# Flip and rotation of the Q and K projection issued one item later, with two qb slots

## The chip, the cores and the metric

The kernel runs on the 8 cores of one Trainium2 chip. Each core computes one batch element; the cores exchange nothing. The metric is the device time of the slowest core in microseconds.

## The reference

Two transformer layers over x of shape (8, 2048, 1024). Cut to what matters here, layer 1's attention:

```python
xn = _layernorm(x, axis=-1)
q = jnp.einsum('bsm,hmd->bshd', xn, W_Q) + b_Q      # 32 heads of 32
k = jnp.einsum('bsm,hmd->bshd', xn, W_K) + b_K
v = jnp.einsum('bsm,hmd->bshd', xn, W_V) + b_V
q = _apply_rotary(q, sin, cos, 32)   # x*cos + flip(x)*sin
k = _apply_rotary(k, sin, cos, 32)
# 16 virtual keys and values, masked softmax, out-projection
```

`flip` swaps the two halves of each head's 32 features, with a minus sign on one. Ahead of this lie layer 0 (a Taylor-feature attention and a mixture of 8 experts of width 4096, every expert computed for every token); behind it layer 1's feed-forward with ternary weights.

## The kernel before

All stages are written out in order by one Python program; each of the engines (TE is TensorE, VE VectorE, SE ScalarE, GE GpSimd's queue, SY SyncE's queue) runs its own instructions strictly in the order written. `barrier()` makes all five wait for everything issued so far. `use_bank` makes TensorE wait until the last reader of that PSUM bank is done. `mm.mark` and `vv.mark` raise a semaphore at the end of a TensorE or VectorE instruction, and `wait` on the returned token waits for that count.

`l1_attn` begins, after a barrier, with the Q and K projection, L908 to L971. xnT, the normalised input, lies in SBUF as 8 tiles of 128 features by 2048 tokens. `which` is 0 for Q and 1 for K. For each, a 4 MB weight matrix is loaded in one DMA from the POOL queue into Wb, converted to bf16 (L920; the helper's line is L224). The second load waits until all matmuls on the first are done (t_Wuse, L966). Then 32 items follow: 8 blocks a2 of 128 output features by 4 chunks cch of 512 tokens. One item is:

- L929: eight matmuls 128x128 by 128x512 that add up in PSUM bank 0 or 1 (tile pA), in turn
- L936 (Q) or L941 (K), VectorE: the eviction, adding the bias (and scaling Q) into the bf16 buffer qb, of which there is one. It waits for the matmuls and for the rotation of the item before, the last reader of qb
- L949: one matmul of qb with the constant pflip, into bank 2 or 3 (tile pB)
- L954: rt1 = qb * cos; L957: rt2 = flipped (in PSUM) * sin; L961: rt1 + rt2 into qrotT or krotT. They wait for L949

A VectorE drain stands ahead of L936/L941, L954 and L961. Each item's instructions are issued completely before those of the next. After the 64 items a small DMA loads the virtual keys (no wait of its own), a barrier follows, and then the V projection (L996, L1000, L1005), the attention proper (L1068 to L1114) and the feed-forward (L1196, L1210) run.

Of the kernel before, what the change touches and what calls it, by code (L numbers as in the profile page):

```python
# [9 lines left out]
BF16 = mybir.dt.bfloat16  # L10
AX = mybir.AxisListType.X
OP = mybir.AluOpType
# [3 lines left out]
DT = 8  # L16
# [5 lines left out]
L1QSC = 32.0 ** -0.5  # L22
# [84 lines left out]
def build(T=2048, upto=99, debug=(), l0sub=9):  # L107
    NT = T // 128
    NCH = T // 512
# [14 lines left out]
    wqf1 = dt("L1_WQ", [D, D], F32, kind="ExternalInput").ap()  # L124
    wkf1 = dt("L1_WK", [D, D], F32, kind="ExternalInput").ap()
# [37 lines left out]
    def sbl(st, name, shape, ty):  # L163
        _uniq[0] += 1
        return st.enter_context(nc.sbuf_tensor(f"{name}_{_uniq[0]}", list(shape), ty))

    xnT = st_xn.enter_context(nc.sbuf_tensor("xnT", [128, DT, T], BF16, side="right"))
    acc = st_acc.enter_context(nc.sbuf_tensor("acc", [128, NT, D], F32, side="right"))

    consts = {nm: es.enter_context(nc.sbuf_tensor("s_" + nm, [p_, f_], ty))  # L170
              for nm, (p_, f_, ty) in CSHAPES.items()}
# [6 lines left out]
    bq_c = es.enter_context(nc.sbuf_tensor("bq_c", [128, 8], F32))  # L178
    bk_c = es.enter_context(nc.sbuf_tensor("bk_c", [128, 8], F32))
# [6 lines left out]
    PS = [pA[:, 0:512], pA[:, 512:1024], pB[:, 0:512], pB[:, 512:1024],  # L186
          pC[:, 0:512], pC[:, 512:1024], pD[:, 0:512], pD[:, 512:1024]]
    bank_free = [None] * 8
# [3 lines left out]
    gw = Sem(es, nc, "gw", dma=True)  # L192
# [7 lines left out]
    mm = Sem(es, nc, "mm")  # L200
    vv = Sem(es, nc, "vv")
    sc = Sem(es, nc, "sc")
# [7 lines left out]
    tk = {}  # L210
    final_outs = []

    with es, nc.Block() as block:
        @block.sync
        def _(sync_unused):
            TE = Eng(nc.tensor)
            VE = Eng(nc.vector)
            SE = Eng(nc.scalar)
            GE = Eng(nc.gpsimd)
            SY = Eng(nc.sync)  # L220

            def dma(q, sem, out, in_, deps=(), **kw):
                q.wait(*deps)
                return sem.mark(q.raw.dma_start(out=out, in_=in_, **kw), 16)  # L224

            def use_bank(bk):
                TE.wait(bank_free[bk])
# [21 lines left out]
            with ExitStack() as st0:  # L249
# [22 lines left out]
                for a in range(DT):  # L272
                    VE.raw.tensor_scalar(out=wq_b[:, a, :], in0=wqf[:, a, 0:128],
                                         scalar1=gamma_c[:, a:a + 1], scalar2=QSC,
                                         op0=OP.mult, op1=OP.mult)
                    tk["wfold"] = vv.mark(VE.raw.tensor_scalar(
                        out=wkv_b[:, a, :], in0=wqf[:, a, 128:384],
                        scalar1=gamma_c[:, a:a + 1], scalar2=None, op0=OP.mult))
                with ExitStack() as st00:
                    wrtmp = sbl(st00, "wrtmp", (128, DT, 8), F32)  # L280
                    for a in range(DT):
                        small_transpose(wrT[:, a, :], wrtmp[:, a, :], a % 2, 8, 128,
                                        deps=(t_wr,))
                    VE.raw.drain()
                    tk["wr"] = vv.mark(VE.raw.tensor_copy(wr_b[:], wrtmp[:]))
                for e in range(8):
                    small_transpose(b1row[:, e, :], b1c0[:, e, :], 2 + e % 2, 32, 128,
                                    deps=(t_b1r,))
# [613 lines left out]
            def l1_attn():  # L902
                st_l1 = ExitStack()
                qrotT = sbl(st_l1, "qrotT", (128, 8, T), BF16)
                krotT = sbl(st_l1, "krotT", (128, 8, T + VKV), BF16)
                v_ext = sbl(st_l1, "v_ext", (128, NT + 1, 32, 65), BF16)
                with st_l1:
                    with ExitStack() as st:  # L908
                        sincos = sbl(st, "sincos", (128, 2, T), BF16)
                        Wb = sbl(st, "Wqk", (128, DT, D), BF16)  # L910
                        qb = sbl(st, "qb", (128, 512), BF16)
                        rt1 = sbl(st, "rt1", (128, 512), BF16)
                        rt2 = sbl(st, "rt2", (128, 512), BF16)
                        tk["sc"] = dma(GE, gd, sincos[:, 0, :], sin_in)
                        tk["sc"] = dma(GE, gd, sincos[:, 1, :], cos_in)
                        t_W = None
                        t_Wuse = None
                        t_qb_used = None
                        for which in range(2):
                            t_W = dma(GE, gw, Wb[:], (wqf1 if which == 0 else wkf1)  # L920
                                      .rearrange("(a p) m -> p a m", p=128), deps=(t_Wuse,))
                            dstT = qrotT if which == 0 else krotT
                            for a2 in range(8):
                                for cch in range(NCH):
                                    bk = (a2 * NCH + cch) % 2
                                    use_bank(bk)
                                    TE.wait(t_W)
                                    for a in range(DT):
                                        t_pq = mm.mark(TE.raw.matmul(  # L929
                                            PS[bk], lhsT=Wb[:, a, a2 * 128:(a2 + 1) * 128],  # L930
                                            rhs=xnT[:, a, cch * 512:(cch + 1) * 512],
                                            start=(a == 0), stop=(a == DT - 1)))
                                    VE.wait(t_pq, t_qb_used)
                                    VE.raw.drain()
                                    if which == 0:
                                        t_evq = vv.mark(VE.raw.tensor_scalar(  # L936
                                            out=qb[:], in0=PS[bk],
                                            scalar1=bq_c[:, a2:a2 + 1], scalar2=L1QSC,
                                            op0=OP.add, op1=OP.mult))
                                    else:  # L940
                                        t_evq = vv.mark(VE.raw.tensor_scalar(  # L941
                                            out=qb[:], in0=PS[bk],
                                            scalar1=bk_c[:, a2:a2 + 1], scalar2=None,
                                            op0=OP.add))
                                    bank_free[bk] = t_evq
                                    bk2 = 2 + (a2 * NCH + cch) % 2
                                    use_bank(bk2)
                                    TE.wait(t_evq, tk["consts"])
                                    t_fl = mm.mark(TE.raw.matmul(  # L949
                                        PS[bk2], lhsT=consts["pflip"][:], rhs=qb[:],  # L950
                                        start=True, stop=True))
                                    VE.wait(t_fl, tk["sc"])
                                    VE.raw.drain()
                                    VE.raw.tensor_tensor(  # L954
                                        out=rt1[:], in0=qb[:],
                                        in1=sincos[:, 1, cch * 512:(cch + 1) * 512], op=OP.mult)
                                    VE.raw.tensor_tensor(  # L957
                                        out=rt2[:], in0=PS[bk2],
                                        in1=sincos[:, 0, cch * 512:(cch + 1) * 512], op=OP.mult)
                                    VE.raw.drain()  # L960
                                    t_rot = vv.mark(VE.raw.tensor_tensor(  # L961
                                        out=dstT[:, a2, cch * 512:(cch + 1) * 512],
                                        in0=rt1[:], in1=rt2[:], op=OP.add))
                                    bank_free[bk2] = t_rot
                                    t_qb_used = t_rot
                            t_Wuse = mm.tok()  # L966
                        tk["rotdone"] = vv.tok()
                        tk["vk"] = dma(GE, gd, krotT[:, :, T:T + VKV],
                                       vk1.rearrange("(a p) m -> p a m", p=128),
                                       allow_slow_non_contiguous=True)  # L970
                        barrier()  # L971

                    with ExitStack() as st:
# [8 lines left out]
                                       deps=(t_vz, t_vo))  # L982
                        t_WVuse = None
                        for half in range(2):
# [3 lines left out]
                                       deps=(t_WVuse,))  # L988
                            for kvt in range(NT):
                                for hc2 in range(2):  # L990
                                    hc = half * 2 + hc2
                                    bk = 4 + (kvt * 2 + hc2) % 4
                                    use_bank(bk)
                                    TE.wait(t_WV, t_bv)
                                    for a in range(DT):
                                        TE.raw.matmul(  # L996
                                            PS[bk], lhsT=xnT[:, a, kvt * 128:(kvt + 1) * 128],
                                            rhs=WVb[:, a, hc2 * 512:(hc2 + 1) * 512],
                                            start=(a == 0), stop=False)
                                    t_pv = mm.mark(TE.raw.matmul(  # L1000
                                        PS[bk], lhsT=ones_row_bf[:],
                                        rhs=bv_r[0:1, hc * 512:(hc + 1) * 512],
                                        start=False, stop=True))
# [19 lines left out]
                    with ExitStack() as st:  # L1023
# [20 lines left out]
                        for cch in range(NCH):  # L1044
# [6 lines left out]
                                        deps=(t_wob_used,))  # L1051
                            for a2 in range(8):
# [4 lines left out]
                                for p in range(nsteps + 1):  # L1057
                                    if p < nsteps:
# [4 lines left out]
                                        sl = p % 2  # L1063
                                        for hh in range(4):
# [5 lines left out]
                                                lhsT=krotT[hb:hb + 32, a2,  # L1070
                                                           kvt * 128:kvt * 128 + rows],
                                                rhs=qrotT[hb:hb + 32, a2,
                                                          cch * 512:(cch + 1) * 512],
                                                start=True, stop=True,
# [255 lines left out]
```

How the kernel before makes its waits and increments, by code:

```python
    def mark(self, instr, n=1):  # L77
        instr.then_inc(self.h, n)
        self.v += n
        return (self, self.v)
# [10 lines left out]
    def wait(self, *deps):  # L91
        for d in deps:
            if d is None:
                continue
            if isinstance(d, (list, tuple)) and d and isinstance(d[0], (list, tuple, type(None), Sem)) \
                    and not (len(d) == 2 and isinstance(d[0], Sem)):
                self.wait(*d)
                continue
            sem, val = d
            if sem.dma:
                val = sem.v
            if val > self.seen.get(sem, 0):
                self.raw.wait_ge(sem.h, val)
                self.seen[sem] = val
```

## Time and profile before

| | us |
|---|---|
| median of 3 runs | 8478.11 |
| the three runs | 8478.11, 8134.01, 8685.17 |
| the profiled execution | 8134.01 |
| its span on the slowest core (core 7) | 8132.4 |
| spans of the eight cores | 8082.8 to 8132.4 |

The profile is of the execution that took 8134.01 us, on its slowest core. PE is TensorE's matmuls, PEld its weight loads, DVE VectorE, ACT ScalarE, POOL GpSimd. A matmul's end is modelled; successive matmuls overlap, so the distance from start to start tells their rate. Idle time of an engine matters only where the chain of waits runs through it.

### The profile page before, as it was taken

The page shows a single profiled execution, that of the slowest core. Times are in us where ns is not written, and L with a number is a line of the kernel's source. Part 1 is how long each engine was busy: PE and PEld are TensorE (multiplying, and loading weights), DVE is VectorE, ACT ScalarE, POOL GpSimd, SP SyncE. Part 2 cuts the span into 40 slices and gives each one's busy share as a digit, 9 for nine tenths or more (in the row PEclk, how much of TensorE's full clock was granted, in tenths as well). Part 3 has the DMA queues.
Part 4 walks back from the last instruction along what each step waited for, and adds up shares of the span by engine and source line. Part 5 has one row for each costly group of instructions (what it writes and reads, how often), then busy time and mean ns, then how long its engine had stood idle before and what let it go on. Part 6 is the DMA issues. An engine that isn't in the chain of part 4 may idle for free.

```text
span 8132.4 us, 72354 instructions; the slowest of 8 cores (8082.8 to 8132.4 us)
## 1 busy us (share of the span) xinstructions
PE 6021.8 (74%) x25392; PEld 2488.6 (31%) x25392; DVE 2372.5 (29%) x4977; ACT 1739.0 (21%) x2768; POOL 152.4 (2%) x177
## 2 busy tenths in 40 slices
PE   3354899999998877887877777936656567676687
PEld 1111344444433333333333333412211122221233
DVE  4633222222222222222222222246343422323000
ACT  1000111111111111111111111100043546474121
POOL 0000000000000000000000000000000000000000
PEclk9555899999999988998988888959866777777898
DMA  1000323323322122112132112020112020201423
GB/s 51 4 0 1 64 45 63 63 45 65 83 55 52 37 52 57 37 34 55 29 62 47 42 39 51 10 57 11 21 36 32 1 32 1 32 1 16 128 66 81
DMA packets 165181, 336.80 MB, mean 41 GB/s; under 512 B 13171, under 2 KB 54940, under 8 KB 162404
## 3 DMA queue, kind: packets, MB, share of 16 engines
q0 software_dynamic: 107888, 221.31, 15.6%
q1 hardware_dynamic: 56948, 110.85, 4.3%
q8 instruction: 220, 3.60, 0.2%
q14 instruction: 125, 1.02, 0.0%
HBM read 445.96 MB, written 46.14 MB: 61 GB/s over the span
## 4 chain that ended last, share of the span: by engine, by line
PE 66%; DMA 11%; DVE 9%; ACT 6%; issue 6%; DVEq 2%; SPq 0%; POOL 0%; ACTq 0%; POOLq 0%
PE pA L706 22%; PE pB L722 11%; PE pC L722 11%; ACT expT L1077 4%; PE pA L1196 3%; DMA denM<-den_stg 2%; DMA wbuf<-L_W 2%; DMA w1t_sc<-buf 2%; PE pB L1210 1%; PE pA L929 1%; PE pC L1210 1%; PE pD L620 1%; PE pC L1099 1%; PE pA L1068 1%; DVE zT L1114 1%
## 5 line engine op out<-in xcount | busy, mean ns | idle before, releaser
L706 PE MATMUL pA<-xnT,W1q 128*128 128x512 bf16 x8192 | 1820.2, 384 | 0.0
L711 ACT ACTIVATE h<-pA,b1c 128x512 bf16<-128x512 f32 x1024 | 703.8, 687 | 3713.7 <-PE pA L706 3713.7
L706 PEld LDWEIGHTS pA<-xnT,W1q 128*128 128x128 bf16 x8192 | 808.1, 99 | 986.2 <-issue 46.3
L736 DVE SCALAR_TENSOR_TENSOR acc<-pB,G,acc 128x512 f32<-128x512 f32 x512 | 383.5, 751 | 2240.7 <-PE pB L722 1640.5
L722 PE MATMUL pB<-W2q,h 128*128 128x512 bf16 x4096 | 936.8, 379 | 124.9 <-ACT h L711 120.0
L722 PE MATMUL pC<-W2q,h 128*128 128x512 bf16 x4096 | 937.6, 379 | 0.0
L722 PEld LDWEIGHTS pB<-W2q,h 128*128 128x128 bf16 x4096 | 383.5, 98 | 637.7 <-issue 207.5
L1077 ACT ACTIVATE expT<-pA,shcol 128x512 bf16<-128x512 f32 (+1 forms) x704 | 462.3, 736 | 414.9 <-PE pA L1068 358.5
L736 DVE SCALAR_TENSOR_TENSOR acc<-pC,G,acc 128x512 f32<-128x512 f32 x512 | 384.0, 751 | 537.9 <-PE pC L722 349.9
L722 PEld LDWEIGHTS pC<-W2q,h 128*128 128x128 bf16 x4096 | 390.3, 98 | 482.1 <-issue 29.0
L1084 DVE TENSOR_TENSOR expT<-expT,s_masks 128x512 bf16<-128x512 bf16 (+1 forms) x640 | 270.4, 425 | 809.6 <-ACT expT L1077 791.9
L771 PE MATMUL pD<-s_ident,wbuf 128*128 128x128 f32 x512 | 116.3, 383 | 495.7 <-DMA w2t_sc<-buf 168.8
L1077 ACT ACTIVATE expT<-pB,shcol 128x512 bf16<-128x512 f32 (+1 forms) x704 | 465.7, 749 | 0.0
L1068 PE MATMUL pA<-qrotT,krotT 32*128 32x512 bf16 (+1 forms) x704 | 191.9, 469 | 343.8 <-DVE zT L1114 309.5
L1068 PE MATMUL pB<-qrotT,krotT 32*128 32x512 bf16 (+1 forms) x704 | 272.1, 460 | 59.7 <-ACT expT L1077 49.2
L1099 PE MATMUL pC<-expT,v_ext 128*65 128x512 bf16 (+1 forms) x704 | 282.9, 487 | 3.8 <-DVE expT L1084 1.5
L1099 PE MATMUL pD<-expT,v_ext 128*65 128x512 bf16 (+1 forms) x704 | 262.7, 454 | 11.8 <-DVE expT L1084 11.6
L1196 PE MATMUL pA<-xnb,w1tb 128*128 128x512 bf16 x1024 | 223.2, 381 | 43.9 <-DMA w1tb<-w1t_sc 43.5
L776 DVE TENSOR_SCALAR ttmp<-pD,thrc 128x128 bf16<-128x128 f32 x512 | 144.3, 344 | 354.3 <-PE pD L771 345.2
L771 PEld LDWEIGHTS pD<-s_ident,wbuf 128*128 128x128 f32 x512 | 83.1, 196 | 527.1 <-issue 524.5
L1068 PEld LDWEIGHTS pA<-qrotT,krotT 32*128 32x128 bf16 (+1 forms) x704 | 41.7, 94 | 542.8 <-issue 541.2
L355 PE MATMUL pA<-s_ident,ln_xtmp 128*128 128x128 f32 x256 | 84.9, 435 | 159.9 <-DVE ln_xtmp L347 128.3
(253 smaller groups left out, 3621.9 us busy)
## 6 DMA issues: line engine op xcount, KB each, us to landing
W1q<-L_W POOLq DMA_DIRECT2D x32, 2048.0 KB, 18.7
W2q<-L_W POOLq DMA_DIRECT2D x32, 2048.0 KB, 32.4
wbuf<-L_W SPq DMA_DIRECT2D x32, 1024.0 KB, 12.0
w2tb<-w2t_sc POOLq DMA_DIRECT2D x8, 4096.0 KB, 17.5
wbuf<-L_W SPq DMA_DIRECT2D x32, 512.0 KB, 10.5
wbuf<-L_W SPq DMA_DIRECT2D x64, 256.0 KB, 4.9
WOb<-L_WO POOLq DMA_DIRECT2D x8, 2048.0 KB, 15.4
o<-stg POOLq DMA_DIRECT2D x64, 256.0 KB, 4.1
```

The source lines that it names most:

```text
L706: t_p1 = mm.mark(TE.raw.matmul(PS[bk], lhsT=W1q[:, s, a, ft * 128:(ft + 1) * 128], rhs=xnT[:, a, tq * 512:(tq + 1) * 512], start=(a == 0), ...
L711: bank_free[bk] = sc.mark(SE.raw.activation(h1[:, ft, :], PS[bk], ACT.Relu, bias=b1c0[:, e, qq * 8 + ft:qq * 8 + ft + 1]))
L722: ins = TE.raw.matmul(PS[bk], lhsT=h1[:, ft, ts_ * 128:(ts_ + 1) * 128], rhs=W2q[:, s, ft, dch * 512:(dch + 1) * 512], start=(ft == 0), st ...
L736: bank_free[bk] = vv.mark(VE.raw.scalar_tensor_tensor(out=aslc, in0=PS[bk], scalar=G[:, tq * 4 + ts_, e:e + 1], in1=aslc, op0=OP.mult, op1 ...
L771: tr = mm.mark(TE.raw.transpose(PS[bk][:, i4 * 128:(i4 + 1) * 128], s_ap, ident32[:]))
L776: VE.raw.tensor_scalar(out=ttmp[:, i4, :], in0=PS[bk][:, i4 * 128:(i4 + 1) * 128], scalar1=thrc[:, thc + 1:thc + 2], scalar2=None, op0=OP. ...
L1068: t_s = mm.mark(TE.raw.matmul(PS[hh][0:rows, :], lhsT=krotT[hb:hb + 32, a2, kvt * 128:kvt * 128 + rows], rhs=qrotT[hb:hb + 32, a2, cch * 5 ...
L1077: t_ex = sc.mark(SE.raw.activation(expT[0:rows, 2 * hh + sl, :], PS[hh][0:rows, :], ACT.Exp, bias=shcol[0:rows, :]))
L1084: t_ex = vv.mark(VE.raw.tensor_tensor(out=expT[0:rows, 2 * hh + sl, :], in0=expT[0:rows, 2 * hh + sl, :], in1=s_masks[0:rows, delta // 128 ...
L1099: t_z[hh] = mm.mark(TE.raw.matmul(PS[4 + hh][0:65, :], lhsT=v_ext[0:rows, kvt, h, :], rhs=expT[0:rows, 2 * hh + sl, :], start=(pz == 0), s ...
L1196: t_p1 = mm.mark(TE.raw.matmul(PS[bk], lhsT=w1tb[:, a, fc * 128:(fc + 1) * 128], rhs=xnb[:, a, tq * 512:(tq + 1) * 512], start=(a == 0), s ...
L1210: TE.raw.matmul(PS[bk], lhsT=hbuf[:, fc, qt * 128:(qt + 1) * 128], rhs=w2tb[:, ws, fc, :], start=(fc == 0), stop=False)
```

## The change

The 64 items are put in one list, and the loop runs over p from 0 to 64. At p it issues the eight matmuls and the eviction of item p, and then the flip matmul and the rotation of item p-1. qb gets two slots, p%2; t_pq, t_evq and t_qb_used are kept per slot. The second weight load is issued at p = 32 and waits for the last matmul of L929 on the first weights, not for all of TensorE's work. rt1 and rt2 stay single. The operations, their shapes and their number are the same.

```diff
-                        qb = sbl(st, "qb", (128, 512), BF16)
+                        qb = sbl(st, "qb", (128, 2, 512), BF16)
...
-                        for which in range(2):
-                            t_W = dma(GE, gw, Wb[:], (wqf1 if which == 0 else wkf1)
-                                      .rearrange("(a p) m -> p a m", p=128), deps=(t_Wuse,))
-                            dstT = qrotT if which == 0 else krotT
-                            for a2 in range(8):
-                                for cch in range(NCH):
-                                    bk = (a2 * NCH + cch) % 2
...
+                        items = [(w_, a2_, c_) for w_ in range(2)
+                                 for a2_ in range(8) for c_ in range(NCH)]
+                        nit = len(items)
+                        half = nit // 2
+                        for p in range(nit + 1):
+                            if p < nit:
+                                which, a2, cch = items[p]
+                                if p % half == 0:
+                                    t_W = dma(GE, gw, Wb[:],
+                                              (wqf1 if which == 0 else wkf1)
+                                              .rearrange("(a p) m -> p a m", p=128),
+                                              deps=(t_Wuse,))
+                                sl = p % 2
+                                bk = p % 2
+                                use_bank(bk)
+                                TE.wait(t_W)
+                                for a in range(DT):
+                                    t_pq[sl] = mm.mark(TE.raw.matmul(
+                                        PS[bk], lhsT=Wb[:, a, a2 * 128:(a2 + 1) * 128],
+                                        rhs=xnT[:, a, cch * 512:(cch + 1) * 512],
+                                        start=(a == 0), stop=(a == DT - 1)))
+                                if p == half - 1:
+                                    t_Wuse = t_pq[sl]
+                                VE.wait(t_pq[sl], t_qb_used[sl])
+                                VE.raw.drain()
+                                if which == 0:
+                                    t_evq[sl] = vv.mark(VE.raw.tensor_scalar(
+                                        out=qb[:, sl, :], in0=PS[bk],
+                                        scalar1=bq_c[:, a2:a2 + 1], scalar2=L1QSC,
+                                        op0=OP.add, op1=OP.mult))
...
+                                bank_free[bk] = t_evq[sl]
+                            if p >= 1:
+                                which, a2, cch = items[p - 1]
+                                sl1 = (p - 1) % 2
+                                dstT = qrotT if which == 0 else krotT
+                                bk2 = 2 + (p - 1) % 2
+                                use_bank(bk2)
+                                TE.wait(t_evq[sl1], tk["consts"])
+                                t_fl = mm.mark(TE.raw.matmul(
+                                    PS[bk2], lhsT=consts["pflip"][:], rhs=qb[:, sl1, :],
+                                    start=True, stop=True))
+                                VE.wait(t_fl, tk["sc"])
+                                VE.raw.drain()
+                                VE.raw.tensor_tensor(
+                                    out=rt1[:], in0=qb[:, sl1, :],
+                                    in1=sincos[:, 1, cch * 512:(cch + 1) * 512], op=OP.mult)
+                                VE.raw.tensor_tensor(
+                                    out=rt2[:], in0=PS[bk2],
+                                    in1=sincos[:, 0, cch * 512:(cch + 1) * 512], op=OP.mult)
+                                VE.raw.drain()
+                                t_rot = vv.mark(VE.raw.tensor_tensor(
+                                    out=dstT[:, a2, cch * 512:(cch + 1) * 512],
+                                    in0=rt1[:], in1=rt2[:], op=OP.add))
+                                bank_free[bk2] = t_rot
+                                t_qb_used[sl1] = t_rot
```

## Rows read from the trace of the kernel before

**Rows 1.** The page: busy times, chain by line, a group (us busy, mean ns | idle before).
```profile
PE 6021.8 (74%) x25392; PEld 2488.6 (31%) x25392; DVE 2372.5 (29%) x4977; ACT 1739.0 (21%) x2768; POOL 152.4 (2%) x177
...
PE pA L706 22%; PE pB L722 11%; PE pC L722 11%; ACT expT L1077 4%; PE pA L1196 3%; DMA denM<-den_stg 2%; DMA wbuf<-L_W 2%; DMA w1t_sc<-buf 2%; PE pB L1210 1%; PE pA L929 1%; PE pC L1210 1%; PE pD L620 1%; PE pC L1099 1%; PE pA L1068 1%; DVE zT L1114 1%
...
L736 DVE SCALAR_TENSOR_TENSOR acc<-pB,G,acc 128x512 f32<-128x512 f32 x512 | 383.5, 751 | 2240.7 <-PE pB L722 1640.5
```

**Rows 2.** Timeline, items 0, 2, 34, 63: start, length, engine, operation, count [idle before <-releaser].
```profile
5464.99 3.57 PE L929 MATMUL pA<-xnT,Wqk 128*128 128x512 bf16 x8 [44.77 <-DMA Wqk<-L_WQ]
...
5476.85 0.75 DVE L936 TENSOR_SCALAR qb<-pA,bq_c 128x512 bf16<-128x512 f32 x1 [0.28 <-PE pA L929]
...
5599.42 0.75 DVE L941 TENSOR_SCALAR qb<-pA,bk_c 128x512 bf16<-128x512 f32 x1 [0.28 <-PE pA L929]
...
5693.41 0.75 DVE L941 TENSOR_SCALAR qb<-pA,bk_c 128x512 bf16<-128x512 f32 x1 [0.28 <-PE pA L929]
...
5695.94 0.43 DVE L961 TENSOR_TENSOR krotT<-rt,rt 128x512 bf16<-128x512 bf16 x1
```

**Rows 3.** Waits, 5400 to 5700 us: who <- for whom, us in total, times, longest.
```profile
POOL Wqk L224 <- PE pB L949: 124.3, 1, 124.3
...
DVE rt L954 <- PE pB L949: 42.8, 63, 0.9
PE pB L949 <- DVE qb L936: 37.0, 32, 1.5
```

**Rows 4.** Timeline of one steady item of Q and the next eviction.
```profile
5499.80 0.75 DVE L936 TENSOR_SCALAR qb<-pA,bq_c 128x512 bf16<-128x512 f32 x1 [0.28 <-PE pA L929]
...
5500.70 0.38 PE L949 MATMUL pB<-qb,s_pflip 128*128 128x512 bf16 x1 [1.13 <-DVE qb L936]
...
5500.91 1.89 PE L929 MATMUL pA<-xnT,Wqk 128*128 128x512 bf16 x8
5501.23 0.42 DVE L954 TENSOR_TENSOR rt<-qb,sincos 128x512 bf16<-128x512 bf16 x1 [0.67 <-PE pB L949]
5501.57 0.68 DVE L957 TENSOR_TENSOR rt<-pB,sincos 128x512 bf16<-128x512 f32 x1
5502.33 0.42 DVE L961 TENSOR_TENSOR qrotT<-rt,rt 128x512 bf16<-128x512 bf16 x1
5503.03 0.75 DVE L936 TENSOR_SCALAR qb<-pA,bq_c 128x512 bf16<-128x512 f32 x1 [0.28 <-PE pA L929]
```

**Rows 5.** Timeline of the last items of Q and the load of K's weights.
```profile
5564.78 0.75 DVE L936 TENSOR_SCALAR qb<-pA,bq_c 128x512 bf16<-128x512 f32 x1 [0.28 <-PE pA L929]
...
5570.89 0.43 DVE L961 TENSOR_TENSOR qrotT<-rt,rt 128x512 bf16<-128x512 bf16 x1 [0.43 <-issue]
5571.47 0.75 DVE L936 TENSOR_SCALAR qb<-pA,bq_c 128x512 bf16<-128x512 f32 x1 [0.16 <-DVE qrotT L961]
...
5572.37 0.38 PE L949 MATMUL pB<-qb,s_pflip 128*128 128x512 bf16 x1 [1.36 <-DVE qb L936]
...
5573.30 0.89 POOL L224 DMA_DIRECT2D Wqk<-L_WK  x1 [124.29 <-PE pB L949]
...
5587.26 3.57 PE L929 MATMUL pA<-xnT,Wqk 128*128 128x512 bf16 x8 [14.52 <-DMA Wqk<-L_WK]
```

**Rows 6.** Groups by line and form, 5400 to 5700 us: rotation and eviction (us busy, mean ns).
```profile
L957 DVE TENSOR_TENSOR rt<-pB,sincos 128x512 bf16<-128x512 f32 x64 | 43.8, 684 | 0.0
...
L936 DVE TENSOR_SCALAR qb<-pA,bq_c 128x512 bf16<-128x512 f32 x32 | 24.0, 751 | 58.8 <-PE pA L929 58.7 <-DVE qrotT L961 0.2
```

**Rows 7.** Windows: us, busy (and count) by engine, granted clock (PEclk), DMA share, GB/s.
```profile
5475.00:5568.00 93.00, 60.48 (x260) 23.17 (x258) 63.10 (x115) 0.00 (x0) 0.00 (x0) 1.00 0.00 1
...
5764.00:5820.00 56.00, 56.00 (x235) 20.57 (x235) 18.05 (x26) 0.00 (x0) 0.00 (x0) 1.00 0.00 1
```

More of the change, by code:

```diff
@@ L917, in l1_attn @@
                         t_Wuse = None
-                        t_qb_used = None
-                        for which in range(2):
-                            t_W = dma(GE, gw, Wb[:], (wqf1 if which == 0 else wkf1)
-                                      .rearrange("(a p) m -> p a m", p=128), deps=(t_Wuse,))
-                            dstT = qrotT if which == 0 else krotT
-                            for a2 in range(8):
-                                for cch in range(NCH):
-                                    bk = (a2 * NCH + cch) % 2
[L926 to L966, printed above, removed]
@@ new lines, in l1_attn @@
+                        t_pq = [None, None]
+                        t_evq = [None, None]
+                        t_qb_used = [None, None]
+                        items = [(w_, a2_, c_) for w_ in range(2)
[28 more added lines that the diff above has]
+                                        op0=OP.add, op1=OP.mult))
+                                else:
+                                    t_evq[sl] = vv.mark(VE.raw.tensor_scalar(
+                                        out=qb[:, sl, :], in0=PS[bk],
+                                        scalar1=bk_c[:, a2:a2 + 1], scalar2=None,
+                                        op0=OP.add))
+                                bank_free[bk] = t_evq[sl]
[23 more added lines that the diff above has]
+                                t_qb_used[sl1] = t_rot
```

## The prediction

> **What bounds the kernel now.** I read the page first. TensorE is busy 6021.8 of 8132.4 us, and the chain that ended last runs mainly through the expert matmuls L706 and L722, with L929, a line of the changed loop, at 1% [rows 1]. So the changed stage is a small part, and the first question is how long it is. The timeline answers: its first matmul starts at 5464.99 us and its last rotation ends at 5695.94 + 0.43 = 5696.37 us [rows 2], a stage of 231.4 us, 2.8% of the span. Barriers stand on both sides of it, so nothing else of the kernel overlaps it, and what it loses or gains moves the end one for one.
>
> Next the stage's waits: TensorE waits 37.0 us for the 32 evictions of Q before their flips (as long again for K), and VectorE waits 42.8 us for the flips [rows 3]. That is a ring. One steady item shows it [rows 4]. Call the eviction E, the flip F, the rotation's three operations R1, R2, R3, the eight matmuls mm. E starts at 5499.80, F at 5500.70, mm of the next item at 5500.91 for 1.89 us, and the next E at 5503.03. The period is 3.23 us = 0.90 (E and hand-off) + 0.21 (F until mm can start) + 1.89 (mm) + 0.23 (hand-off). The rotation, 5501.23 to 5502.75, lies beside mm and ends 0.28 us before E. TensorE idles 1.13 us in each item because F sits at once behind its own E.
>
> **The change part by part.** (a) *F and R go one item later.* TensorE's order becomes mm(p), F(p-1), mm(p+1), F(p); VectorE's E(p), R(p-1), E(p+1), R(p). The ring is opened: mm(p+1) needs E(p-1) (its bank, and F(p-1) ahead of it in the queue), not E(p). Two engine sums then compete.
>
> TensorE: the eight matmuls take 1.89 us including the end of the last, 0.379 long, so they start (1.89 - 0.38)/7 = 0.216 us apart; nine of them are 1.94 us per item.
>
> VectorE, from start to start: E to R1 0.75 + 0.08 = 0.83 (the 0.08 is the gap a drain leaves between R2, 0.68 long, and R3, which starts 0.76 after it); R1 to R2 0.34; R2 to R3 0.76 [rows 4]; R3 to the next E 0.58, from the one place where E waited for the rotation in front of it, 5570.89 to 5571.47 [rows 5]. That wait stays: slot p%2 was last read by R(p-2), which is the operation directly ahead of E(p). Sum 2.51 us. VectorE is the bound, and the period falls from 3.23 to 2.51.
>
> Is the loop free of other rings at 2.51? Put E(p-1) at 0. It is seen at 0.90; F(p-1) starts, mm(p+1) starts at 1.11 and ends at 3.00; E(p+1) is due at 5.02. R1(p-1) is due behind E(p), at 2.51 + 0.83 = 3.34, and F needs 0.53 us until R1 can start (5500.70 to 5501.23), so it is ready at 1.43. Slack is 1.8 us or more on both sides: that is the cover of F and mm. Without it, each would again cost its 1.1 us per item.
>
> Do VectorE's operations keep their durations when matmuls write other banks beside them? R2 reads PSUM beside mm in all but the last item of each half and has 684 ns throughout [rows 4, 6]; E reads PSUM with TensorE idle now, 751 ns. The expert stage has 512 accumulations from PSUM at the same 751 ns while TensorE works nearly without a gap [rows 1]. I take no stretch.
>
> Sum over periods. Items 2 to 29 of Q: 5564.78 - 5476.85 = 87.9 us, becoming 27 x 2.51 = 67.8, gain 20.2. Items 2 to 31 of K: 5693.41 - 5599.42 = 94.0, becoming 29 x 2.51 = 72.8, gain 21.2 [rows 2, 5].
>
> (b) *Starts at the low clock.* The first matmuls of each half run at the lower of TensorE's two levels, 1.2 GHz: eight take 3.57 us, starts (3.57 - 0.58)/7 = 0.427 apart [rows 2]. TensorE then no longer waits for E between the first groups. Q: mm(0), mm(1), F(0), about three low and five fast matmuls of mm(2), hand-offs: 3.42 + 3.42 + 0.43 + 1.28 + 1.08 + 0.39 = 10.0 us until E(2) against 5476.85 - 5464.99 = 11.9; gain 1.9. K likewise with F(31) in front: 10.4 against 5599.42 - 5587.26 = 12.2; gain 1.8 [rows 2, 5]. The moment of the rise is taken as in the profile, some 8 to 9 us in.
>
> (c) *The load of WK.* It now waits for the last matmul of Q, not for the last flip. Before: E(29) at 5564.78, load issued at 5573.30, 8.52 us. After: mm(31) follows F(29), so it ends 0.90 + 0.21 + 1.89 = 3.00 us after E(29); the queue needs 5573.30 - (5572.37 + 0.38) = 0.55. Gain 8.52 - 3.55 = 5.0 us [rows 5]. The load itself takes 5587.26 - 5573.30 = 13.96 us as before, with nothing else moving. F(31) now stands behind mm(32) and so behind this load; R(31) is late by 14 us, but only E(33) needs its slot, and it is done by then. The virtual-key load behind WK on the POOL queue moves with it and has no reader before the barrier.
>
> (d) *The end.* One more rotation trails the last E: 0.83 + 0.34 + 0.76 + 0.50 + 0.34 + 0.76 + 0.43 = 3.96 us, against 5696.37 - 5693.41 = 2.96 now. Loss 1.0. The wider qb costs nothing but memory.
>
> Sum: 20.2 + 21.2 + 1.9 + 1.8 + 5.0 - 1.0 = 49.1 us. The profiled execution took 8134.0 us, 1.6 beyond its span; 8134.0 - 49.1 = **8085 us**. The median of the three runs shown, 8478.1, is 344 us higher than the one profiled; the sum is for an execution like the profiled one, and the ratio, 0.994, carries over.
>
> *Bounds of the period.* Unseen so far are E followed by a drain and a wait already met, and 60 back-to-back items. Lower end: durations alone, less the 0.08 by which R2 starts before R1 ends, 0.75 + 0.42 + 0.68 + 0.42 - 0.08 = 2.20 us, gain 49.1 + 56 x 0.31 = 66.5. Upper end: a hand-off as if from another engine, 0.28 us, on both sides of E: 0.75 + 0.28 + 0.34 + 0.76 + 0.42 + 0.28 = 2.83, gain 49.1 - 56 x 0.32 = 31.2. I take 2.51 since its two gaps come from this loop's own instructions.
>
> **The rivals.** *A. VectorE has no gaps beyond its durations.* The period is 0.75 + 0.42 + 0.68 + 0.42 = 2.28 us, the gain 49.1 + 56 x 0.23 = 62 us, the time 8072. For it: these four durations are fixed within 2 ns. Against: R3 to E took 0.58, not 0.42 [rows 5]. The Trainium skill, VectorE: DVE Perf Modes, "The DRAIN you can't avoid", states this rule: a next operation starts when the pipe is empty, and a semaphore costs nothing extra; by it the time would be 8072. The trace agrees only in part: R2 starts 0.08 us before R1 ends, and a semaphore of the operation in front did cost 0.16.
>
> *B. Dear waits on VectorE*, the upper end above: 8103. For it: each item has three waits and three drains in a strict queue. Against: a drain shows 0.08.
>
> *C. The change doesn't overlap.* If something keeps mm(p+1) from starting until E(p) is seen, F and R moved but the ring stays at about 3.2 us; 8134. For it: nothing I find; bank p%2 is freed by E(p-2), and both flip banks by R(p-3). Against: the same matmuls run without pause in the V projection, TensorE busy 56.00 of 56.00 us [rows 7].
>
> *D. TensorE falls to 1.2 GHz: slower.* Nine matmuls at 0.427 make 3.84 us per item, above today's 3.23. All 64 items: 32 x 3.42 + 30 x 0.43 + 0.7 + 14.0 + 32 x 3.84 + 3.3 = 263 us against 231.4, so 8134 + 32 = 8166. It decides from the point where the mean item passes 3.23: (3.23 - 2.51)/(3.84 - 2.51) = 54% of the items at the low level. Against: the stage's granted clock is 1.00 (2.4 GHz) with TensorE paused 1.13 us in every item, and 1.00 again where it is packed [rows 7]; the change lies between the two. The Trainium skill, TensorE: Matmul & The Clock Gate, "A second HAM failure mode: psum-queue depth-cycling", warns that short idle moments between 512-column groups cycling through banks can make the clock swing. If it held here the time would go toward 8166; the 1.00 of the present loop, which has longer pauses, speaks against it.
>
> **How the numbers follow.** Main case 0.60 (8085), A 0.12 (8072), B 0.17 (8103), C 0.07 (8134), D 0.04 (8166). Main, A and B hold 0.89, between 8068 and 8103. An execution's other 7900 us also vary; the two longest cores lie at 8131.9 and 8132.4, the others down to 8082.8. I widen to **8055 to 8128**. About 2%, 163 us, is what a measurement of this kernel can tell from no change. Even a TensorE-bound loop (1.94 us) would gain 7.7 + 87.9 + 94.0 - 56 x 1.94 = 81 us, and D loses 32, so all cases are within 2%: faster 0.02, same 0.96, slower 0.02 for what I have not seen.
>
> **What would show it.** Period of E to E 2.51 us (A: 2.28, B: 2.83, C: 3.2, D: 3.8); VectorE idle below 0.3 us per item, no longer waiting for flips; TensorE's wait for E of item p-1 about 0.6 us per item; WK issued some 81 us after the first matmul, not 108; stage 182 us instead of 231; granted clock 1.00. The prediction is wrong if E stretches beyond 0.75 us beside matmuls, if R1 still waits for F, or if a later stage is longer by tens of us.

## The result and the profile after

| us | before | after |
|---|---|---|
| profiled execution | 8134.0 | 8081.9 |
| its span, slowest core (7) | 8132.4 | 8080.1 |
| median of 13 runs | 8469.9 | 8131.8 |
| ratio after / before | | 0.9935, 95% interval 0.9911 to 0.9958 |
| the changed stage, core 7 | 231.4 | 181.4 |
| the changed stage, mean of 8 cores | 229.7 | 180.9 |

The change is faster by 0.65%, clear of the noise but well inside 2%. In some executions of either kernel the cores of one die, or of both, ran at a lower granted clock for part of the time and took up to 10% longer; the ratio leaves those out, the two medians do not.

In the changed kernel the matmuls are L938, the eviction L947 (Q) and L952 (K), the flip L964, the rotation L969, L972 and L976. First its chain by line, from the page: the expert matmuls still lead, and the line of the changed loop, L929 with 1% before, is no longer in the list.

```profile
PE pA L706 22%; PE pB L722 11%; PE pC L722 11%; ACT expT L1091 4%; PE pA L1210 3%; DMA denM<-den_stg 2%; DMA wbuf<-L_W 2%; DMA w1t_sc<-buf 2%; PE pB L1224 2%; PE pC L1224 1%; PE pD L620 1%; PE pC L1113 1%; PE pA L1082 1%; DVE zT L1128 1%; DVE den_stg L1125 1%
```

The timeline of one steady item and the next eviction, core 7, answers [rows 4]:

```profile
5489.25 0.75 DVE L947 TENSOR_SCALAR qb<-pA,bq_c 128x512 bf16<-128x512 f32 x1 [0.16 <-DVE qrotT L976]
5490.09 0.42 DVE L969 TENSOR_TENSOR rt<-qb,sincos 128x512 bf16<-128x512 bf16 x1
...
5490.14 0.38 PE L964 MATMUL pB<-qb,s_pflip 128*128 128x512 bf16 x1 [0.43 <-DVE qb L947]
...
5490.36 1.89 PE L938 MATMUL pA<-xnT,Wqk 128*128 128x512 bf16 x8
5490.43 0.68 DVE L972 TENSOR_TENSOR rt<-pB,sincos 128x512 bf16<-128x512 f32 x1
5491.19 0.42 DVE L976 TENSOR_TENSOR qrotT<-rt,rt 128x512 bf16<-128x512 bf16 x1
5491.77 0.75 DVE L947 TENSOR_SCALAR qb<-pA,bq_c 128x512 bf16<-128x512 f32 x1 [0.16 <-DVE qrotT L976]
```

Eviction to eviction is 2.52 us where it was 3.23. VectorE runs end to end: its steps from start to start are 0.84, 0.34, 0.76 and 0.58. What ends its idle time ahead of the eviction is now the rotation in front of it, no longer TensorE. The pause of TensorE before each flip has shrunk from 1.13 to 0.43 us.

The waits of the stage, 5380 to 5640 us (who waits for whom, us in total, times, longest), answer [rows 3]. The line "rt <- PE pB" of 42.8 us is gone: no rotation waits for a flip. The waits of TensorE for evictions fell from 37.0 and 36.4 to 11.7 and 14.4.

```profile
PE pA L938 <- DMA Wqk<-L_WQ: 45.0, 1, 45.0
...
PE pB L964 <- DVE qb L952: 14.4, 29, 2.2
...
PE pA L938 <- DMA Wqk<-L_WK: 13.8, 1, 13.8
PE pB L964 <- DVE qb L947: 11.7, 28, 0.4
DVE qb L947 <- DVE qrotT L976: 4.4, 28, 0.2
DVE qb L952 <- DVE krotT L976: 4.4, 28, 0.2
```

Groups by form (us busy, mean ns), answering [rows 6], and a window in the middle of Q, answering [rows 7]: no operation of VectorE was stretched, and the granted clock stayed at 1.00 (2.4 GHz).

```profile
L972 DVE TENSOR_TENSOR rt<-pB,sincos 128x512 bf16<-128x512 f32 x64 | 43.7, 683 | 0.0
...
L947 DVE TENSOR_SCALAR qb<-pA,bq_c 128x512 bf16<-128x512 f32 x32 | 24.0, 750 | 54.5 <-PE pA L938 50.1 <-DVE qrotT L976 4.4
```

```profile
5460.00:5525.00 65.00, 54.40 (x234) 20.88 (x232) 56.64 (x104) 0.00 (x0) 0.00 (x0) 1.00 0.00 1
```

The timeline of the points from which the stage is summed: first matmul, third eviction, 30th eviction, load of K's weights, start of K, 35th and last eviction, last rotation.

```profile
5447.91 5.81 PE L938 MATMUL pA<-xnT,Wqk 128*128 128x512 bf16 x16 [44.95 <-DMA Wqk<-L_WQ]
...
5456.40 0.75 DVE L947 TENSOR_SCALAR qb<-pA,bq_c 128x512 bf16<-128x512 f32 x1 [0.16 <-PE pA L938]
...
5524.62 0.75 DVE L947 TENSOR_SCALAR qb<-pA,bq_c 128x512 bf16<-128x512 f32 x1 [0.16 <-DVE qrotT L976]
...
5528.18 0.89 POOL L224 DMA_DIRECT2D Wqk<-L_WK  x1 [96.12 <-PE pA L938]
...
5542.18 3.57 PE L938 MATMUL pA<-xnT,Wqk 128*128 128x512 bf16 x8 [13.75 <-DMA Wqk<-L_WK]
...
5551.61 0.75 DVE L952 TENSOR_SCALAR qb<-pA,bk_c 128x512 bf16<-128x512 f32 x1 [0.16 <-DVE krotT L976]
...
5625.35 0.75 DVE L952 TENSOR_SCALAR qb<-pA,bk_c 128x512 bf16<-128x512 f32 x1 [0.16 <-DVE krotT L976]
...
5628.91 0.42 DVE L976 TENSOR_TENSOR krotT<-rt,rt 128x512 bf16<-128x512 bf16 x1
```

| core 7, us | before | after | gain | forecast |
|---|---|---|---|---|
| start to third eviction | 11.86 | 8.49 | 3.4 | 1.9 |
| 27 periods of Q | 87.93 | 68.22 | 19.7 | 20.2 |
| 30th eviction to the load of WK | 8.52 | 3.56 | 5.0 | 5.0 |
| the load of WK | 13.96 | 14.00 | 0.0 | 0 |
| start of K to its third eviction | 12.16 | 9.43 | 2.7 | 1.8 |
| 29 periods of K | 93.99 | 73.74 | 20.3 | 21.2 |
| last eviction to last rotation | 2.96 | 3.98 | -1.0 | -1.0 |
| stage | 231.4 | 181.4 | 50.0 | 49.1 |

What lies around the stage differs by more than most of these terms. On core 7 the part ahead of it was 17.1 us shorter (5465.0 to 5447.9) and the part behind it 14.8 us longer (2436.0 to 2450.8). Over the eight cores little of that is left: ahead 5452.1 and 5450.9 in the mean, behind 2431.3 and 2434.4. So the stage is read from its own ends on eight cores, not from the span.

### The profile page after: what moved, and what is told of

Same layout as the page of the kernel before. It is cut to its first block, busy times and chain, and to the rows that moved or that the text cites. A ratio compares the mean times of both kernels' runs of the same rounds, so it can differ in the third digit from the quotient of the medians.

```text
span 8080.1 us, 72415 instructions; the slowest of 8 cores (8046.7 to 8080.1 us)
## 1 busy us (share of the span) xinstructions
PE 6036.8 (75%) x25392; PEld 2494.9 (31%) x25392; DVE 2373.3 (29%) x4977; ACT 1737.1 (21%) x2768; POOL 152.4 (2%) x177
## 4 chain that ended last, share of the span: by engine, by line
PE 65%; DMA 11%; DVE 10%; ACT 6%; issue 6%; DVEq 3%; SPq 0%; POOL 0%; ACTq 0%; POOLq 0%
PE pA L706 22%; PE pB L722 11%; PE pC L722 11%; ACT expT L1091 4%; PE pA L1210 3%; DMA denM<-den_stg 2%; DMA wbuf<-L_W 2%; DMA w1t_sc<-buf 2%; PE pB L1224 2%; PE pC L1224 1%; PE pD L620 1%; PE pC L1113 1%; PE pA L1082 1%; DVE zT L1128 1%; DVE den_stg L1125 1%
## 5 line engine op out<-in xcount | busy, mean ns | idle before, releaser
L1113 PE MATMUL pD<-expT,v_ext 128*65 128x512 bf16 (+1 forms) x704 | 257.2, 445 | 12.0 <-DVE expT L1098 11.7
```

The lines of the kernel that those rows point to most:

```text
L1113: t_z[hh] = mm.mark(TE.raw.matmul(PS[4 + hh][0:65, :], lhsT=v_ext[0:rows, kvt, h, :], rhs=expT[0:rows, 2 * hh + sl, :], start=(pz == 0), s ...
```

## The experiments

All give the same quantities, each a mean over the eight cores of the profiled execution unless it says otherwise: the stage, from its first matmul to its last rotation, and the period, the distance from eviction to eviction (items 4 to 29 of Q, 6 to 31 of K). Before: stage 229.7, period 3.26 and 3.24. After: 180.9, 2.53 and 2.55. On two cores of most traces the record of the stage's first matmul is missing; there 0.43 us, the distance of the next ones, is added. Of the kernels below only the last was timed in enough executions to compare its time with that of the kernel before (12 and 17); the others had one to four each and are read by stage and period alone.

**Was it a ring before, and is it VectorE now?** The flip is issued three times, the first two overwritten by the third. In the kernel before:

```diff
+                                    for _rep in range(2):
+                                        TE.raw.matmul(
+                                            PS[bk2], lhsT=consts["pflip"][:], rhs=qb[:],
+                                            start=True, stop=True)
```

> The kernel before with each flip issued three times instead of once (two more 128x512 matmuls per item, 0.43 us at 0.216 each). Theory (before was a ring through TensorE and the eviction, with VectorE 0.28 us short of binding): the period goes from 3.24 to 3.24 + 0.43 = 3.67 us, the stage from 231 to about 231 + 64 x 0.43 = 259 us. Rival (VectorE was the bound before already): period stays near 3.24, stage near 232.

Measured: period 3.69 and 3.68, stage 257.5. All of the added 0.43 us lands in the period. The same edit in the kernel after:

> The kernel after with each flip issued three times. TensorE's sum per item becomes 11 x 0.216 = 2.37 us. Theory (VectorE is the bound now, TensorE has 0.58 us of slack): period stays at 2.53 us, stage 181 to about 184 us (the few items at the low clock pay 0.85 each). Rival (a ring through TensorE still sets the period, rival C's kind): period 2.53 + 0.43 = 2.96, stage 209.

Measured: period 2.53 and 2.54, stage 181.4, within 0.5 us of the kernel after. The timeline of core 5 shows three flips in the place of one and the period unchanged, 5491.59 to 5494.12:

```profile
5491.59 0.75 DVE L947 TENSOR_SCALAR qb<-pA,bq_c 128x512 bf16<-128x512 f32 x1 [0.16 <-DVE qrotT L980]
...
5492.49 0.59 PE L965 MATMUL pB<-qb,s_pflip 128*128 128x512 bf16 x2
...
5492.92 0.38 PE L968 MATMUL pB<-qb,s_pflip 128*128 128x512 bf16 x1
...
5494.12 0.75 DVE L947 TENSOR_SCALAR qb<-pA,bq_c 128x512 bf16<-128x512 f32 x1 [0.16 <-DVE qrotT L980]
```

What bounded before does not bound any more, and rival C is out: TensorE's own work per item can grow to 2.37 us (11 x 0.216) at no cost.

**What does the wait for the operation directly ahead cost?** The kernel after with three slots:

```diff
-                        qb = sbl(st, "qb", (128, 2, 512), BF16)
+                        qb = sbl(st, "qb", (128, 3, 512), BF16)
...
-                                sl = p % 2
+                                sl = p % 3
...
-                                sl1 = (p - 1) % 2
+                                sl1 = (p - 1) % 3
```

> The kernel after with three slots of qb instead of two, so that an eviction waits for the rotation before the one directly ahead of it. Theory (0.08 of the 0.16 us between rotation and eviction is the semaphore of the operation directly ahead): period 2.53 - 0.08 = 2.45, stage 181 - 5 = 176 us. Rival A in full (VectorE has no gaps when no semaphore is awaited): 2.28, stage 167. Rival (the wait costs nothing, the gap is the drain and the queue's wait instruction): 2.53, stage 181.

Measured: period 2.48 in both halves, stage 177.5. The gap between rotation and eviction falls from 0.16 to 0.10 us (core 3, 5490.28 + 0.42 to 5490.80):

```profile
5490.28 0.42 DVE L976 TENSOR_TENSOR qrotT<-rt,rt 128x512 bf16<-128x512 bf16 x1
5490.80 0.75 DVE L947 TENSOR_SCALAR qb<-pA,bq_c 128x512 bf16<-128x512 f32 x1
```

Nearly every item took 2.46 us where the kernel after takes 2.52 or 2.53; the mean of 2.48 holds one or two longer items per half as well, of 2.55 to 2.82 us. So that wait costs 0.06 to 0.07 us per item, 3.4 us in all, and a gap of 0.10 us stays, with a drain and a wait already met between the two. It lies between the theory (0.08) and the rival (nothing). Rival A's 2.28 is out: with no wait left on the operation directly ahead, VectorE still needs 2.46.

**Was it the order or VectorE's load?** The kernel before, order unchanged, with the eviction on ScalarE:

```diff
-                                    VE.wait(t_pq, t_qb_used)
-                                    VE.raw.drain()
-                                    if which == 0:
-                                        t_evq = vv.mark(VE.raw.tensor_scalar(
...
+                                    SE.wait(t_pq, t_qb_used, t_bqs)
+                                    t_evq = sc.mark(SE.raw.activation(
+                                        qb[:], PS[bk], ACT.Identity,
+                                        bias=(bq_s if which == 0 else bk_c)[:, a2:a2 + 1],
+                                        scale=L1QSC if which == 0 else 1.0))
```

> The kernel before, order unchanged, with the eviction (bias and scale) as one activation on ScalarE instead of VectorE. Theory (the ring bounds, whichever engine evicts): period = 1.89 + 0.23 + about 0.69 + 0.15 + 0.21 = 3.17 us, stage about 227 us, VectorE idle more. Rival (the order doesn't matter, VectorE's load of 2.3 us per item did): period falls below 2.5, stage below 185.

Measured: period 3.09 and 3.11, stage 219.5. Taking a third of VectorE's work away leaves the period above 3; the ring holds. Its terms can be read on core 4:

```profile
5490.13 0.69 ACT L938 ACTIVATE qb<-pA,bq_s 128x512 bf16<-128x512 f32 x1 [2.40 <-PE pA L933]
...
5490.96 0.38 PE L946 MATMUL pB<-qb,s_pflip 128*128 128x512 bf16 x1 [0.98 <-ACT qb L938]
...
5491.18 1.89 PE L933 MATMUL pA<-xnT,Wqk 128*128 128x512 bf16 x8
...
5493.22 0.69 ACT L938 ACTIVATE qb<-pA,bq_s 128x512 bf16<-128x512 f32 x1 [2.40 <-PE pA L933]
```

0.83 + 0.22 + 1.89 + 0.15 = 3.09. The 0.08 us by which it beat the expected 3.17 is the hand-off from TensorE, 0.15 to ScalarE against 0.23 to VectorE.

The same edit in the kernel after:

> The kernel after with the eviction as one activation on ScalarE. Theory (VectorE is the bound of the changed loop; without its eviction its sum is about 1.7 us, so TensorE's 9 x 0.216 = 1.94 us bounds): period 1.94, stage = 8.3 + 29 x 1.94 + 0.3 + 14.0 + 9.1 + 29 x 1.94 + 2.9 = 147 us. Rival (a ring through the hand-offs sets 2.5): stage near 181. Rival (no overlap of the engines at all): about 3.1, as in the order before.

Measured: period 1.94 in both halves on all cores, stage 146.7. With the order changed and VectorE relieved, TensorE is the bound: nine matmuls times 0.216. The two edits together are worth 83.0 us of stage (229.7 to 146.7), alone 48.9 and 10.2: relieving VectorE pays only once the ring is open.

**The load of K's weights.** The kernel before with only the condition of that load changed:

```diff
-                            t_Wuse = mm.tok()
+                            t_Wuse = t_pq
```

> The kernel before, with only the second load's condition changed: it waits for the last matmul on Q's weights and not for the last flip. Theory: the load is issued 1.8 us earlier relative to the last eviction of Q (from 1.8 us behind E(31) to about 0.3 behind it), stage 231 - 1.6, period unchanged at 3.24. Rival (the early release makes a good part of the gain): stage shorter by 5 us or more.

Measured: on core 7 the load is issued 0.1 us behind the start of the last eviction of Q instead of 1.8, stage 227.8, shorter by 1.9 us, period unchanged. From the last eviction of Q to the first of K it is 1.6 us less (19.4 to 17.8), which is this edit's share; the rest comes from the starts of the halves, which differ from run to run. The other 3.3 of the 5.0 us that the changed kernel gains at this point come from the matmuls running ahead of the evictions, as the forecast had it.

The kernel after with the load in eight parts, each issued when its 128 columns of Q's weights are done:

```diff
+                                if p < half and cch == NCH - 1:
+                                    kk = a2 // 7
+                                    t_K[kk] = dma(
+                                        GE, gks[kk], Wb[:, :, a2 * 128:(a2 + 1) * 128],
+                                        wkf1.rearrange("(a p) m -> p a m", p=128)
+                                        [:, :, a2 * 128:(a2 + 1) * 128],
+                                        deps=(t_pq[sl],))
```

> The kernel after with the load of K's weights split into eight loads of 128 columns, each issued as soon as the last matmul on that part of Q's weights is done. Theory: the 14 us stall and the second start at the low clock vanish; E(31) to E(32) 16.3 becomes 2.5, E(32) to E(34) 5.5 becomes 5.05; stage 181 - 14 = 167 us. Rival (the finer rows land late): a stall remains before item 32 and the stage lies between 167 and 181. Rival (the loads slow VectorE or TensorE beside them): period of Q above 2.53.

Measured: stage 167.5, period 2.53 and 2.55, last eviction of Q to first of K 2.88 us instead of 16.2. The stall is gone, and the loads slow nothing beside them. That one item is 0.35 us above a period: VectorE pauses 0.45 us ahead of a rotation for nothing that the profile shows.

**All together.** Both edits on the kernel after:

> Both edits: eviction on ScalarE and K's weights in eight loads. Theory: stage = 8.3 + 61 x 1.94 + 2.9 = 130 us, 51 less than the kernel after and 101 less than the kernel before; time about 8082 - 51 = 8031 us, ratio to the kernel before 0.987. Rival (other parts of the kernel give it back): the stage as said, the time above 8060.

In the profiled execution the granted clock of the stage was 1.00 on cores 4 and 5, where it took 129.9 and 129.8 us, and 0.81 to 0.83 on the other six, where it took 151 to 156. With TensorE as the bound the lower clock goes straight into the period: 2.36 us where it lasted. So the same kernel ran again:

> The kernel of both edits once more, for its time and for a profile of it at the full granted clock. Theory: period 1.94 us, stage 130 us on every core, time 51 us below the kernel after and 101 us below the kernel before, ratio to before 0.987 to 0.988. Rival (the rest of the kernel gives part of it back): stage 130 us, ratio above 0.990.

Measured: period 1.94, stage 129.9 (129.2 to 130.2 over the cores), profiled execution 8024.7 us, ratio to the kernel before 0.9894, interval 0.9842 to 0.9947. The window of core 7 shows what bounds it: TensorE has no idle moment in 110 us, and the eight loads lie beside it.

```profile
5470.00:5580.00 110.00, 110.00 (x511) 49.88 (x510) 82.11 (x171) 39.17 (x57) 6.99 (x8) 1.00 0.22 20
```

The stage is 99.8 us shorter than before, and what lies around it is where it was (5449.5 ahead and 2431.6 behind in the mean, 5452.1 and 2431.3 before). The interval of the ratio holds both the theory's 0.987 and the rival's 0.990, so from the time alone it is not decided whether some tenths of a per cent are given back; the profiled execution gives nothing back (8134.0 to 8024.7, 109 us). It is faster than the kernel before. Against the kernel after its time was not measured side by side: the stage is 51.0 us shorter, and the profiled executions took 8081.9 and 8024.7.

## Why the prediction was right or wrong

**The number.** 8085 was forecast and the profiled execution took 8081.9, but the measured median, 8131.8, lies 3.8 us above the range of 8055 to 8128. The step that failed is the range in "How the numbers follow", with the sentence before it in the sum, "the sum is for an execution like the profiled one". I had read that the three runs of before were 8134, 8478 and 8685 and that the median was 344 us higher, and still built the range from one kind of execution: terms of the stage and the spans of eight cores in one profile. The scatter between executions was put at nothing, without a reason.

What the runs showed in its place: the 13 executions of the kernel after are seven of 8076.7 to 8131.8 us and six of 8378.7 to 8884.4. The median is the longest of the seven, an execution in which one die (cores 4 to 7, 8089.5 to 8130.1 us, granted clock 0.837 to 0.840) was behind the other (8043.8 to 8074.6, 0.843 to 0.845). The middle of the seven is 8081.9. Of the kernel before, six took 8134.0 to 8160.0 and seven 8469.9 to 8900.3, so its median is the shortest of the seven long ones. The miss of 3.8 us is luck too: had one of the seven been a long one, the median would have been 8378.7 or more; had one of the six been short, it would most likely have been inside the range. The cause of the scatter is not known beyond the lower granted clock that goes with it.

The change in the time was right: 0.9935 measured, 0.994 forecast; 49.1 us forecast for the stage, 50.0 on core 7 and 48.9 in the mean of the cores. That it is so near owes something to luck: on core 7 the starts gave 2.4 us more than forecast and the periods 1.4 less.

**(a) Flip and rotation one item later.** Right. The ring of 3.23 us was the bound before (x1, x4), VectorE's sum is the bound after (x2), and the sum of 2.51 from single rows came out as 2.53 (Q) and 2.55 (K). Nearly every period on core 7 is 2.52 or 2.53 us, 0.01 of it at E to R1 (0.84 where 0.83 was put), and one item of K took 2.98, with 0.61 us of idle time on VectorE ahead of its eviction. Together they are the 1.4 us by which the two periodic terms fell short. The kernel before has four such long items, of 3.5 to 3.6 us; what makes them was not tested. The wait behind R3, read from one row of before, was there in 28 of 32 items of each half. Two of the signs were put a little wrong: the sum itself leaves VectorE 0.31 us idle per item (2.51 less its 2.20), not below 0.3, and with a period of 2.53 it was 0.33; TensorE's pause before a flip was put at 0.6 and is 0.43, because the profile counts the end of the last matmul as busy.

**The Trainium skill's rule of rival A**, VectorE: DVE Perf Modes, "The DRAIN you can't avoid", says that a semaphore costs nothing extra between two operations. Here the trace does not agree: the third slot took 0.06 to 0.07 us off each item. The larger part of the gap, 0.10 of 0.16 us, is not the semaphore's.

**(b) Starts at the low clock.** Right in kind, too small: 3.4 and 2.7 us where 1.9 and 1.8 stood. The forecast kept the moment at which TensorE's clock rises as core 7 shows it before, 8.0 to 9.5 us after the first matmul: its second group still ran at 1.2 GHz nearly to its end (3.39 us for eight, 1.89 at 2.4 GHz). After, its first 16 matmuls follow each other without a pause and take 5.81 us, where at 0.427 us each they would take 7.0, and the first flip is at full speed; the rise came some 4 us sooner. But the same profile of before holds both kinds. On cores 1, 2, 3 and 7 the second group was slow and the third eviction lies 11.9 to 12.1 us behind the first matmul; on cores 0, 4, 5 and 6 the clock had risen by the first flip, 4.6 us in, and it lies at 10.1 to 10.2. K's start shows both kinds too: 10.0 us on cores 0, 1 and 4, 12.2 on the others. First core 7, whose first matmul is at 5464.99, then core 5:

```profile
5469.61 0.58 PE L949 MATMUL pB<-qb,s_pflip 128*128 128x512 bf16 x1 [1.05 <-DVE qb L936]
5469.99 3.39 PE L929 MATMUL pA<-xnT,Wqk 128*128 128x512 bf16 x8
...
5446.40 3.57 PE L929 MATMUL pA<-xnT,Wqk 128*128 128x512 bf16 x8 [46.11 <-DMA Wqk<-L_WQ]
5451.02 0.38 PE L949 MATMUL pB<-qb,s_pflip 128*128 128x512 bf16 x1 [1.05 <-DVE qb L936]
5451.24 1.89 PE L929 MATMUL pA<-xnT,Wqk 128*128 128x512 bf16 x8
```

So the moment of the rise was no constant that one core could give. After, the rise had come on all cores 2.8 to 5.0 us after the first matmul, and the third eviction lies at 7.6 to 8.7 us, where the forecast had 10.0. The other kernels agree: third eviction at 10.1 to 13.0 us, and both kinds of start, in the order of before (x1, x4, y4); 7.4 to 9.1 us, and no late rise, in the order of after (x2, x3, y1, y2, z1). What the missing pause does to the rise was not tested by itself.

**(c) The load of WK.** Right to 0.1 us, and y4 with y2 split it into its parts.

**(d) The end.** Right: 3.98 us against 3.96.

**The rivals.** A fell by x3, B (2.83) by the period, C by x2. D did not occur: the granted clock was 1.00 with pauses of 1.13 us per item (before), of 0.43 us (after), and of none (z1). On the second rule cited, TensorE: Matmul & The Clock Gate, "A second HAM failure mode: psum-queue depth-cycling", the trace does not show the swings that it warns of.

**Same, faster, slower.** 0.96 on same was right: 0.9935. The bound of 81 us from TensorE's own work was sound but for the starts, which were put too small: y1, bound by TensorE, took 83.0 us off the stage.

## What to carry to other kernels

When two engines hand one item back and forth, write the period as the ring of durations and hand-offs, then ask for each engine's own sum; delaying the second half by one item replaces the ring by the larger sum, and the next gain in the period is then on that engine. Give the buffer one slot more than the overlap needs, so that no operation waits for the one directly ahead of it; here that was worth 3.4 us of 181. Read the start of a stage on several cores before taking its clock for granted. And when the runs shown scatter by more than the change, say what the measured figure will be a median of, and let the scatter into the range.

## What the runs showed of the hardware

- From the shown end of a group of matmuls to the start of its reader: 0.23 us on VectorE (5502.80 to 5503.03 before), 0.15 us on ScalarE (x4). From the end of the eviction to the flip on TensorE: 0.15 us from VectorE (before), 0.14 us from ScalarE (x4).
- Two VectorE operations with nothing between them start 0.34 us apart where the first takes 0.42: the second starts 0.08 us before the first is shown to end. A drain between them turns that into a gap of 0.08 us (R2 to R3), a drain and a wait already met into 0.09 to 0.10 (E to R1 after, R3 to E in x3), a drain and a wait on the one directly ahead into 0.16 (R3 to E after).
- A load of 128 columns of K's weights (512 KB in fp32, in rows of 512 bytes) took 4.5 us from issue to landing, and eight of them went beside the matmuls without a change in the period (y2); all 4 MB in one load took 13.9 us (after).
- TensorE's clock at the start of the stage: after a wait of 45 us for the weights it begins at 1.2 GHz on every core. Without a pause behind the first group it had risen by 2.8 to 5.8 us (after, x2, x3, y1, z1); with a pause of 1.05 us there it had risen by 4.6 us on four cores and not before 8.0 us on four (before).
